# Turning a mixed block behind the value product and adding it two steps later, with the first token's value sent round the scans by GpSimd

## The chip, the cores and the metric

The kernel runs on one core of one Trainium2 chip. The metric is the device time of one execution in microseconds, the median of the runs. The engines are TensorE (PE, its weight loads PEld), VectorE (DVE), ScalarE (ACT), GpSimd (POOL) and SyncE (SP, which here issues all transfers).

## The reference

Two transformer layers over `x` (4 batches of 512 tokens, 512 channels) with a context `ctx` of the same shape. The part that the change touches is the first one, called Mix here, a recurrence over the tokens of each channel:

```
def step(carry, kv_t):               # kt = layernorm(x)[t], vt = ctx[t]
    no = max(o, u + kt); A = exp(o - no); E = exp(u + kt - no)
    y = (A * p + E * vt) / (A * q + E)
    ...
x = x + tanh(g_xattn[0]) * wkv(w, u, layernorm(x), ctx)   # Mix
x = x + tanh(g_ffn[0])   * bitlinear_ffn(layernorm(x))
x = x + tanh(g_xattn[1]) * quantized_cross_attention(layernorm(x), ctx)
x = x + tanh(g_ffn[1])   * quantized_projection(layernorm(x))
```

For the first token p and q are zero, so that y is v of that token itself.

## The kernel before, in words

One program per engine is written out by hand; each engine runs its own list in order, and semaphores connect them (`wait_ge` blocks the engine until another has counted far enough). Mix has 16 steps: step s is batch b = s // 4 and block k = s % 4 of 128 channels. Channels lie on the partitions and the 512 tokens along the free axis, so that the sums over earlier tokens are two scans on VectorE, one for the denominator (`DEN`, L1450) and one for the numerator (`NUM`, L1461). Beside the recurrence each step does work for later stages: TensorE makes a block of the keys (L1062, 12 matmuls into bank 6, "key product") and of the values (L1073, 12 matmuls into bank 7, "value product") of the later cross-attention, and the feed-forward weights are signed on ScalarE and turned by transfers.

What the steps of the prediction touch, in the order in which each engine has it in step s:

- TensorE: `key_turn(s+1)` (L1020, L1022), key product of s, `y_turn(s-1)` (L1041: four transposes of the mixed block `YT` into bank 2), value product of s, `context_turn(s+4)` (L1034: four transposes of a context block into bank 1).
- VectorE: for s up to 7 `batch_stats` (L1365, L1366), `ratio(s-1)` (L1397, L1399, L1403, L1404: the block's quotient into `YT`), scan of `DEN` (L1450), `low_context(s+3)` (L1392), `E*v` (L1455), correction of `DEN` (L1458) and a one for the first token (memset L1459), scan of `NUM` (L1461), `values(s-1)` (L1411: bank 7 to SBUF), correction of `NUM` (L1467) and the first token's v (copy L1468), `residual(s-1)` (L1384: bank 2 added to `X`). Steps 11 to 14 end with parts of the preparation of the next stage (L1417 to L1436).
- ScalarE: two copies of the turned context (L711, L713), the signs of the weights (L771), exponentials (L720, L725), the inverse of `DEN` (L732, L734), the key block to SBUF (L780, L784).
- GpSimd: `normed(s+4)` (L549), `numerators(s+1)` (L540), low half of the key (L580).

The token order is shifted by one: column t of `DEN` and `NUM` belongs to token t+1, and the last column (`SEQ - 1`) to token 0. That column is written by L1459 and L1468, and L1403 moves it to column 0 of `YT`.

Three buffers are single. Bank 7: the value product of s waits for `val_sb`, that is for L1411 of step s, which reads the value product of s-1. Bank 2: `y_turn` waits for the residual (`mixed`) of the block before. `YT`: the last instruction of `ratio(s)` waits until the block before has been turned:

```
up_to(dve, yT_ps, s)          # y_turn(s-1) is done
stt(YT[:, 0:1], ...)          # L1403
stt(YT[:, 1:SEQ], ...)        # L1404
```

Of the kernel before, what the change touches and what calls it, by code (L numbers as in the profile page):

```python
# [8 lines left out]
ALU = mybir.AluOpType  # L9
ACT = mybir.ActivationFunctionType  # L10
# [50 lines left out]
def flamingo_kernel(nc, x, ctx_2048, g_xattn, g_ffn, w, u, w1, w2, w3, wq, bq, wkv, bkv, wp, bp, gamma, wl, out):  # L61
    stack = ExitStack()
    with stack:
# [3 lines left out]
        def sem(name):  # L67
            return stack.enter_context(nc.semaphore(name))
# [158 lines left out]
        logs_done, inv_ready, trial_done, first_done = sem("logs_done"), sem("inv_ready"), sem("trial_done"), sem("first_done")  # L227
# [30 lines left out]
        out_done = sem("out_done")  # L258

        NSMALL = 6  # L260
        CONSTS = {"ones": 3, "growth": 3 + DB, "all": 4 + DB}
        ROUNDED, SUMMED = lambda m, k: DB * m + k + (1 if m == 0 else 2), DB + 1
        SETUP = {"vec_ps": 1, "means_ps": 2, "wl_mean_ps": 3}
# [246 lines left out]
        def _(pool):  # L510
# [23 lines left out]
            def numerators(s):  # L534

                k = s % DB
                pool.wait_ge(ctx_vt, s + 1)
                pool.wait_ge(ue_ready, s + 1)
                up_to(pool, num_set, s - 1)
                nc.gpsimd.tensor_tensor(UEV[k % 2], UE[k % 2], VT[:, k, :], ALU.mult).then_inc(uev_ready, 1)  # L540

            def normed(n):

# [25 lines left out]
            for s in range(DB * BATCH):  # L569
                k = s % DB  # L570
                if k == 0 and s + DB < DB * BATCH:
                    deviations(s // DB + 1)
                if s + DB < DB * BATCH:
                    normed(s + DB)
                if s + 1 < DB * BATCH:
                    numerators(s + 1)
                pool.wait_ge(key_f, s + 1)
                pool.wait_ge(key_hi, s + 1)
                up_to(pool, k_out[k % 2], 16 * (s // 2))
                nc.gpsimd.tensor_tensor(KHL[k % 2][:, 1, :], KF, KHL[k % 2][:, 0, :], ALU.subtract).then_inc(key_lo, 1)  # L580
# [108 lines left out]
        def _(act):  # L689
# [16 lines left out]
            def context(n):  # L706

                b, k = divmod(n, DB)
                act.wait_ge(vT_ps, n + 1)
                up_to(act, val_ps, DB * (b - 1))  # L710
                nc.scalar.copy(CH[b % 2][:, k, :], TURNED(n)[:, :]).then_inc(ctx_hi, 1)  # L711
                up_to(act, num_set, n - DB + 1)
# [14 lines left out]
            def inverse(s):  # L727

                act.wait_ge(den_set, s + 1)
                up_to(act, trial_done, s)  # L730
                up_to(act, first_done, s)
                nc.scalar.activation(INV, DEN[:, :], ACT.Ln).then_inc(logs_done, 1)  # L732
                act.wait_ge(logs_done, s + 1)
                nc.scalar.activation(INV, INV, ACT.Exp, scale=-1.0).then_inc(inv_ready, 1)  # L734

            def magnitudes(s):
                act.wait_ge(signs, s + 1)
# [258 lines left out]
        def _(pe):  # L996
# [54 lines left out]
            for s in range(DB * BATCH):  # L1051
                b, k = divmod(s, DB)
                operands = ((WKVH, CH[b % 2]), (WKVL, CH[b % 2]), (WKVH, CL[b % 2]))
                if s + 1 < DB * BATCH:
                    key_turn(s + 1)
                pe.wait_ge(ctx_hi, DB * b + DB)
                up_to(pe, key_f, s)
                for p, j in parts:
                    if p == 2 and j == 0:
                        pe.wait_ge(ctx_lo, DB * b + DB)  # L1060
                    wt, cx = operands[p]
                    last_ = mm(bank[6][:, :], wt[:, j, k * P:k * P + P], cx[:, j, :],  # L1062
                               start=(p == 0 and j == 0), stop=(p == 2 and j == DB - 1))
                last_.then_inc(key_ps, 1)
                if s > 0:
                    if s == 1:
                        pe.wait_ge(ctx_vt, DB)
                        pe.wait_ge(ctx_lo, DB)
                    y_turn(s - 1)
                up_to(pe, val_sb, s)  # L1070
                for p, j in parts:
                    wt, cx = operands[p]
                    last_ = mm(bank[7][:, :], cx[:, j, k * P:k * P + P], wt[:, j, D:2 * D],  # L1073
                               start=(p == 0 and j == 0), stop=(p == 2 and j == DB - 1))
                last_.then_inc(val_ps, 1)
# [257 lines left out]
        def _(dve):  # L1333
# [60 lines left out]
            def ratio(s):  # L1394

                dve.wait_ge(inv_ready, s + 1)
                tt(DEN[:, :], DEN[:, :], INV, ALU.mult).then_inc(trial_done, 1)  # L1397
                dve.wait_ge(num_set, s + 1)
                tt(Y0, NUM[:, :], INV, ALU.mult).then_inc(first_done, 1)  # L1399
                dve.wait_ge(trial_done, s + 1)  # L1400
                dve.wait_ge(first_done, s + 1)
                up_to(dve, yT_ps, s)
                stt(YT[:, 0:1], DEN[:, SEQ - 1:SEQ], 2.0, Y0[:, SEQ - 1:SEQ], ALU.subtract, ALU.mult)  # L1403
                stt(YT[:, 1:SEQ], DEN[:, 0:SEQ - 1], 2.0, Y0[:, 0:SEQ - 1], ALU.subtract, ALU.mult).then_inc(y_ready, 1)  # L1404

            def values(s):
                dve.wait_ge(val_ps, s + 1)
# [34 lines left out]
            for s in range(DB * BATCH):  # L1442
                k = s % DB
                if s + 2 * DB < DB * BATCH:
                    batch_stats(s // DB + 2, k)
                if s > 0:
                    ratio(s - 1)
                dve.wait_ge(e_ready, s + 1)
                up_to(dve, y_ready, s)
                nc.vector.tensor_tensor_scan(DEN[:, :], DEC[:, k:k + 1].to_broadcast([P, SEQ]), E[:, :], 0.0,  # L1450
                                             ALU.mult, ALU.add).then_inc(sums_done, 1)
                if 0 < s and s + DB - 1 < DB * BATCH:
                    low_context(s + DB - 1)
# [4 lines left out]
                stt(DEN[:, 0:SEQ - 1], DEN[:, 0:SEQ - 1], US[:, k:k + 1], UE[k % 2][:, 1:SEQ], ALU.mult, ALU.add)  # L1458
# [8 lines left out]
                stt(NUM[:, 0:SEQ - 1], NUM[:, 0:SEQ - 1], US[:, k:k + 1], UEV[k % 2][:, 1:SEQ], ALU.mult, ALU.add)  # L1467
                nc.vector.tensor_copy(NUM[:, SEQ - 1:SEQ], VT[:, k, 0:1]).then_inc(num_set, 1)  # L1468
                if s > 0:
                    residual(s - 1)  # L1470
                if s == DB * BATCH - 5:
                    prep_stats(0)
                if s == DB * BATCH - 4:
                    prep_max(0)
                    prep_quant(0)
                    prep_stats(1)
                if s == DB * BATCH - 3:
                    prep_scaled(0)
# [333 lines left out]
```

## Time and profile before

| | |
|---|---|
| median of 3 runs | 966.96 us (964.26 to 967.22) |
| the profiled execution | 966.35 us, its span 964.6 us |
| granted TensorE clock, mean of the span | 0.955 |
| Mix, from the first scan (37.82 us) to the last L1041 (190.46 us) | 152.6 us |

The profiled execution lies 0.6 us under the median; its time is 1.75 us above its span. Positions in the rows below are microseconds from the start of the span.

### The profile page before, as it was taken

To read this page: it belongs to the slowest core of one execution; us is meant where nothing else is said; L and a number is where in the kernel's file an instruction comes from. 1 tells how busy PE (TensorE), PEld (TensorE's weight loads), DVE (VectorE), ACT (ScalarE), POOL (GpSimd) and SP (SyncE) were. 2 spreads that over 40 slices of the span, in tenths; PEclk is the share of its full clock that TensorE was granted. 3 is DMA by queue.
4 is the path that set the end of the run, shared out by engine and by line. 5 is a ranking of instruction groups with operands and counts; after the bars stand their busy time and mean duration, and the time that the engine had idled before them with its cause. 6 is when DMAs were issued, how large, how long until landed. Compare 5 with 4: busy or idle time off the path is not lost.

```text
span 964.6 us, 14534 instructions
## 1 busy us (share of the span) xinstructions
PE 821.9 (85%) x4373; PEld 353.2 (37%) x4373; DVE 759.5 (79%) x1510; ACT 576.9 (60%) x974; POOL 487.2 (51%) x560
## 2 busy tenths in 40 slices
PE   2899987789898989899999968799999999974754
PEld 2544443334344444444444432222223232222321
DVE  4699998879899899999998758477777777634884
ACT  3588886543555565666665544466666666655762
POOL 2866663223334444444444343475757575764761
PEclk9999999899999999999999986899999999996886
DMA  8668875533353442352433241212122221000111
GB/s 283 214 178 221 223 204 151 143 88 65 62 115 55 72 103 57 63 70 55 79 65 65 45 100 54 84 49 79 55 77 57 72 61 46 1 1 0 43 66 66
DMA packets 172392, 86.51 MB, mean 90 GB/s; under 512 B 124048, under 2 KB 156960, under 8 KB 172320
## 3 DMA queue, kind: packets, MB, share of 16 engines
q1 hardware_dynamic: 172320, 85.64, 35.6%
q8 instruction: 34, 0.56, 0.2%
q14 instruction: 38, 0.31, 0.1%
HBM read 37.76 MB, written 12.58 MB: 52 GB/s over the span
## 4 chain that ended last, share of the span: by engine, by line
PE 37%; DVE 22%; issue 7%; ACT 6%; SPq 4%; DMA 3%; POOL 0%; ACTq 0%; DVEq 0%
PE bank L1098 10%; PE bank L1190 5%; PE bank L1161 5%; PE bank L1110 4%; PE bank L1180 4%; DMA A<-B 3%; DVE bank L1516 3%; DVE gsm L1518 3%; DVE B L1527 2%; SPq L438 2%; DVE B L1521 2%; PE bank L1307 2%; ACT bank L806 2%; PE bank L1209 2%; PE bank L1199 2%
## 5 line engine op out<-in xcount | busy, mean ns | idle before, releaser
L1098 PE MATMUL bank<-A,B 128*128 128x512 f16 x1024 | 233.0, 381 | 15.8 <-DVE B L1527 15.6
L1642 DVE TENSOR_REDUCE B<-bank 128x1 f32<-128x512 f32 x256 | 168.0, 683 | 73.9 <-PE bank L1161 73.9
L936 ACT ACTIVATE A<-bank 128x512 f32<-128x512 f32 x256 | 144.1, 593 | 106.9 <-PE bank L1180 103.5
L594 POOL TENSOR_TENSOR B<-B 128x512 f16<-128x512 f32 x64 | 76.4, 1193 | 223.4 <-DVE B L1527 147.2
L1098 PEld LDWEIGHTS bank<-A,B 128*128 128x128 f16 x1024 | 98.8, 98 | 142.9 <-DVE B L1527 20.6
L663 POOL TENSOR_TENSOR B<-A 128x512 f32<-128x512 f32 x64 | 79.3, 1269 | 96.0 <-ACT A L936 96.0
L806 ACT ACTIVATE bank<-B 128x512 f32<-128x512 f32 x64 | 38.5, 602 | 137.4 <-DVE B L1521 137.4
L1110 PE MATMUL bank<-A,B 128*128 128x512 f16 x512 | 120.7, 379 | 0.0
L1180 PE MATMUL bank<-A 98*128 98x512 f16 x256 | 94.5, 390 | 21.2 <-ACT A L936 10.5
L1161 PE MATMUL bank<-A 96*128 96x512 f16 x256 | 97.7, 409 | 7.9 <-DMA A<-B 4.7
L663 POOL TENSOR_TENSOR B<-B,A 128x512 f32<-128x512 f32 x64 | 79.0, 1264 | 0.1
L1190 PE MATMUL bank<-A,B 128*32 128x512 f32 x512 | 69.6, 616 | 1.0 <-ACT A L936 1.0
L1110 PEld LDWEIGHTS bank<-A,B 128*128 128x128 f16 x512 | 49.5, 98 | 54.3 <-DMA B<-B 0.4
L1073 PE MATMUL bank<-B 128*128 128x512 f16 x192 | 47.2, 399 | 17.9 <-DVE B L1411 17.9
L1527 DVE SCALAR_TENSOR_TENSOR B<-bank,gsm 128x512 f32<-128x512 f32 x64 | 44.2, 691 | 16.1 <-ACT bank L806 14.0
L1516 DVE SCALAR_TENSOR_TENSOR bank<-bank,ffs,B 128x512 f32<-128x512 f32 x64 | 48.2, 753 | 9.1 <-PE bank L1098 8.6
L1161 PEld LDWEIGHTS bank<-A 96*128 96x128 f16 x256 | 23.3, 100 | 85.0 <-DVE B L1642 65.3
L801 ACT ACTIVATE B<-bank,ffs 128x512 f32<-128x512 f32 x64 | 43.1, 673 | 13.4 <-PE bank L1098 13.1
L549 POOL TENSOR_SCALAR B<-X,mv,rs 128x128 f32<-128x128 f32 x64 | 49.8, 792 | 0.4
L1180 PEld LDWEIGHTS bank<-A 98*128 98x128 f16 x256 | 25.0, 99 | 67.2 <-ACT A L936 36.6
L1062 PE MATMUL bank<-B 128*128 128x512 f16 x192 | 46.1, 392 | 0.0
L1518 DVE TENSOR_REDUCE gsm<-bank 128x8 f32<-128x512 f32 x64 | 44.3, 692 | 2.2
(216 smaller groups left out, 1479.5 us busy)
## 6 DMA issues: line engine op xcount, KB each, us to landing
B<-in_L_ffn_w_dram SPq DMA_DIRECT2D x48, 256.0 KB, 3.4
A<-k_parts SPq DMA_DIRECT2D x48, 128.0 KB, 2.6
A<-B SPq DMA_DIRECT2D x192, 32.0 KB, 1.9
X<-in_x_dram SPq DMA_DIRECT2D x4, 1024.0 KB, 9.4
B<-in_ctx_dram SPq DMA_DIRECT2D x16, 256.0 KB, 4.4
k_parts<-B SPq DMA_DIRECT2D x16, 256.0 KB, 4.3
v_rows<-B SPq DMA_DIRECT2D x16, 256.0 KB, 2.3
B<-v_rows SPq DMA_DIRECT2D x16, 256.0 KB, 3.4
```

Source lines behind the costliest of these rows:

```text
L594: nc.gpsimd.tensor_tensor(HLb[j][:, 1, :], Db[j % 2], HLb[j][:, 0, :], ALU.subtract).then_inc(lo_done, 1)
L663: nc.gpsimd.tensor_tensor(ACC[j], PR[j] if t == 1 else ACC[j], PR[(HG * t + j) % 8], ALU.add).then_inc(acc_done, 1)
L936: nc.scalar.activation(PR[(HG * t + j) % 8], bank[2 + j % 2][:, :], ACT.Exp, scale=SCALE).then_inc(exp_done, 1)
L1098: last = mm(bank[2 * n + q][:, :], XQT[a][:, m, :], wt[:, m % DB, j * 512:j * 512 + 512], start=(m == 0), stop=(m == 2 * DB - 1))
L1110: last = mm(bank[5 + q][:, :], HT[j][:, m, :], W3T[:, DB * j + m % DB, :], start=(j == 0 and m == 0), stop=(j == FC - 1 and m == 2 * DB - 1))
L1161: mm(bank[ROW_BANKS[r % 3]][:, :], QS[0:96, HG * g + j, t * P:t * P + P], KS[0:96, HG * g + j, :], start=True, stop=True).then_inc(row_ps, 1)
L1180: mm(bank[2 + j % 2][:, :], KS[0:98, HG * g + j, t * P:t * P + P], QS[0:98, HG * g + j, :], start=True, stop=True).then_inc(st_ps, 1)
L1190: last_ = mm(bank[6][DH * j:DH * j + DH, :], VB[:, t, (HG * g + j) * DH:(HG * g + j + 1) * DH], PR[(HG * t + j) % 8], start=(t == 0), stop ...
L1516: stt(H, H, C2, SAb[q], ALU.mult, ALU.mult).then_inc(h_done, 1)
L1518: link(reduce(gsm[:, 0, :], grouped(H), AX.X, ALU.max, apply_absolute_value=True))
L1527: stt(grouped(Db[q]), grouped(bank[q][:, :]), RND, spread(1), ALU.subtract, ALU.mult).then_inc(d_done, 1)
L1642: reduce(NMX[g % 2][:, t, j:j + 1], bank[ROW_BANKS[r % 3]][:, :], AX.X, ALU.max, negate=True).then_inc(row_max, 1)
```

## The change

It does three things. In TensorE's list `y_turn(s-1)` moves from ahead of the value product of step s to behind it. In VectorE's list the residual moves from the end of step s (block s-1) to the place between the correction of `DEN` and the scan of `NUM` (block s-2). And token 0 leaves the scans: the memset L1459, the copy L1468 and the one-column L1403 go; GpSimd writes -v of token 0 into column 0 of `UEV`, and a new `first_value` copies it into `YT` column 0. (`YT` holds -y; the residual multiplies by -tanh.) The remaining operations of `ratio` and `inverse` work on 511 columns in place of 512.

```diff
@@ gpsimd
-                nc.gpsimd.tensor_tensor(UEV[k % 2], UE[k % 2], VT[:, k, :], ALU.mult).then_inc(uev_ready, 1)
+                up_to(pool, y_first, s - 1)
+                nc.gpsimd.tensor_scalar(UEV[k % 2][:, 0:1], VT[:, k, 0:1], -1.0, 0.0, ALU.mult, ALU.add)
+                nc.gpsimd.tensor_tensor(UEV[k % 2][:, LATER], UE[k % 2][:, LATER], VT[:, k, LATER],
+                                        ALU.mult).then_inc(uev_ready, 1)
+            def first_value(s):
+                pool.wait_ge(uev_ready, s + 1)
+                up_to(pool, yT_ps, s)
+                nc.gpsimd.tensor_scalar(YT[:, 0:1], UEV[s % 2][:, 0:1], 1.0, 0.0, ALU.mult, ALU.add).then_inc(y_first, 1)
...
+                if s > 0:
+                    first_value(s - 1)
                 if s + DB < DB * BATCH:
                     normed(s + DB)
@@ tensor
             def y_turn(s):
                 pe.wait_ge(y_ready, s + 1)
+                pe.wait_ge(y_first, s + 1)
...
-                if s > 0:
-                    ...
-                    y_turn(s - 1)
                 up_to(pe, val_sb, s)
                 for p, j in parts:
...
                 last_.then_inc(val_ps, 1)
+                if s > 0:
+                    ...
+                    y_turn(s - 1)
                 if s + DB < DB * BATCH:
                     context_turn(s + DB)
@@ vector
-                tt(DEN[:, :], DEN[:, :], INV, ALU.mult).then_inc(trial_done, 1)
+                tt(DEN[:, PAIRED], DEN[:, PAIRED], INV[:, PAIRED], ALU.mult).then_inc(ratio_done, 1)
...
                 up_to(dve, yT_ps, s)
-                stt(YT[:, 0:1], DEN[:, SEQ - 1:SEQ], 2.0, Y0[:, SEQ - 1:SEQ], ALU.subtract, ALU.mult)
-                stt(YT[:, 1:SEQ], DEN[:, 0:SEQ - 1], 2.0, Y0[:, 0:SEQ - 1], ALU.subtract, ALU.mult).then_inc(y_ready, 1)
+                stt(YT[:, LATER], DEN[:, PAIRED], 2.0, Y0[:, PAIRED], ALU.subtract, ALU.mult).then_inc(y_ready, 1)
...
-                nc.vector.memset(DEN[:, SEQ - 1:SEQ], 1.0).then_inc(den_set, 1)
+                if s > 1:
+                    residual(s - 2)
                 dve.wait_ge(ev_ready, s + 1)
                 nc.vector.tensor_tensor_scan(NUM[:, :], ...
...
-                nc.vector.tensor_copy(NUM[:, SEQ - 1:SEQ], VT[:, k, 0:1]).then_inc(num_set, 1)
-                if s > 0:
-                    residual(s - 1)
...
             ratio(DB * BATCH - 1)
+            residual(DB * BATCH - 2)
```

TensorE's list in one step of Mix before, from the end of the key product on (bank 6 key product, bank 2 `y_turn`, bank 7 value product, bank 1 context):

```order
L1062 MATMUL bank6<-B 128x512 [waits ctx_lo]
L1062 MATMUL bank6<-B 128x512 x3
L1041 MATMUL bank2<-id32,B 128x128 [waits mixed,y_ready]
L1041 MATMUL bank2<-id32,B 128x128 x3
L1073 MATMUL bank7<-B 128x512 [waits val_sb]
L1073 MATMUL bank7<-B 128x512 x11
L1034 MATMUL bank1<-id32,B 128x128 [waits ctx_lo,ctx_vt,ctx_in2]
L1034 MATMUL bank1<-id32,B 128x128 x3
```

The same place of the change (its L1077, L1083, L1056 and L1048 are the L1062, L1073, L1041 and L1034 of before; these rows are shown without bank numbers):

```order
L1077 MATMUL bank<-B 128x512 [waits ctx_lo]
L1077 MATMUL bank<-B 128x512 x3
L1083 MATMUL bank<-B 128x512 [waits val_sb]
L1083 MATMUL bank<-B 128x512 x11
L1056 MATMUL bank<-id,B 128x128 [waits mixed,y_first,y_ready]
L1056 MATMUL bank<-id,B 128x128 x3
L1048 MATMUL bank<-id,B 128x128 [waits ctx_lo,ctx_vt,ctx_in2]
L1048 MATMUL bank<-id,B 128x128 x3
```

The four transposes of y have moved behind the value product, and so behind its wait for `val_sb`.

VectorE's list in one step before, from the end of `ratio` to the residual:

```order
L1403 SCALAR_TENSOR_TENSOR B<-bank,B 128x1 [waits yT_ps,first_done,trial_done]
L1404 SCALAR_TENSOR_TENSOR B<-bank,B 128x511
L1450 SCALAR_TENSOR_TENSOR bank<-vec,bank 128x512 [waits y_ready,e_ready]
L1392 TENSOR_TENSOR B<-bank,B 128x512 [waits ctx_vt,ctx_hi]
L1455 TENSOR_TENSOR bank<-bank,B 128x512 [waits ctx_vt]
L1458 SCALAR_TENSOR_TENSOR bank<-bank,vec,B 128x511 [waits ue_ready,sums_done]
L1459 MEMSET bank 128x1
L1461 SCALAR_TENSOR_TENSOR bank<-vec,bank 128x512 [waits ev_ready]
L1411 SCALAR_TENSOR_TENSOR B<-bank,bv_all 128x512 [waits val_ps]
L1467 SCALAR_TENSOR_TENSOR bank<-bank,vec,B 128x511 [waits uev_ready,scans_done]
L1468 COPY bank<-B 128x1
L1384 SCALAR_TENSOR_TENSOR X<-bank,ffs,X 128x4x128 [waits yT_ps]
```

The same place of the change (L1417 is the L1404 of before, L1399 the residual L1384, L1424 the L1411):

```order
L1417 SCALAR_TENSOR_TENSOR B<-bank,B 128x511 [waits yT_ps,ratio_done]
L1463 SCALAR_TENSOR_TENSOR bank<-vec,bank 128x512 [waits y_ready,e_ready]
L1407 TENSOR_TENSOR B<-bank,B 128x512 [waits ctx_vt,ctx_hi]
L1468 TENSOR_TENSOR bank<-bank,B 128x512 [waits ctx_vt]
L1471 SCALAR_TENSOR_TENSOR bank<-bank,vec,B 128x511 [waits ue_ready,sums_done]
L1399 SCALAR_TENSOR_TENSOR X<-bank,ffs,X 128x4x128 [waits yT_ps]
L1476 SCALAR_TENSOR_TENSOR bank<-vec,bank 128x512 [waits ev_ready]
L1424 SCALAR_TENSOR_TENSOR B<-bank,bv_all 128x512 [waits val_ps]
L1482 SCALAR_TENSOR_TENSOR bank<-bank,vec,B 128x511 [waits uev_ready,scans_done]
```

Three one-column instructions are gone and the residual stands ahead of the scan of `NUM`; the wait for `yT_ps` at the end of `ratio` is still there.

## Rows read from the trace of the kernel before

**Rows 1.** Busy time by stretch, steps 2 to 12: PE, PEld, DVE, ACT, POOL, clock
```profile
51.97:150.75 98.78, 89.36 (x478) 48.27 (x476) 94.93 (x172) 81.45 (x126) 60.91 (x71) 1.00 0.77 207
```

**Rows 2.** Waits of Mix: who waited for whom, total us, times, longest
```profile
PE bank L1073 <- DVE B L1411: 17.9, 14, 3.6
```

**Rows 3.** Timeline of one step: start, us, engine, line, operation, idle time and its releaser
```profile
106.67 0.67 DVE L1411 SCALAR_TENSOR_TENSOR B<-bank,bv_all 128x512 f32<-128x512 f32 x1
...
107.41 2.76 PE L1073 MATMUL bank<-B 128*128 128x512 f16 x12 [1.05 <-DVE B L1411]
...
107.92 0.15 DVE L1468 COPY bank<-B 128x1 f32<-128x1 f32 x1
107.98 0.74 DVE L1384 SCALAR_TENSOR_TENSOR X<-bank,ffs,X 128x512 f32<-128x512 f32 x1
...
108.64 0.69 DVE L1397 TENSOR_TENSOR bank<-bank,B 128x512 f32<-128x512 f32 x1
...
109.79 0.57 PEld L1034 LDWEIGHTS bank<-id,B 128*128 128x128 f32 x4
110.00 0.60 PE L1034 MATMUL bank<-id,B 128*128 128x128 f32 x4
110.02 0.16 DVE L1403 SCALAR_TENSOR_TENSOR B<-bank,B 128x1 f32<-128x1 f32 x1
110.09 0.68 DVE L1404 SCALAR_TENSOR_TENSOR B<-bank,B 128x511 f32<-128x511 f32 x1
110.33 1.16 POOL L580 TENSOR_TENSOR B<-B 128x512 f16<-128x512 f32 x1 [3.06 <-ACT B L780]
...
110.64 0.58 ACT L711 CAST B<-bank 128x512 f16<-128x512 f32 x1 [0.44 <-PE bank L1034]
...
111.12 0.59 ACT L713 COPY B<-bank 128x512 f32<-128x512 f32 x1
...
112.01 0.67 DVE L1392 TENSOR_TENSOR B<-bank,B 128x512 f16<-128x512 f32 x1
...
113.86 1.22 DVE L1461 TENSOR_TENSOR_SCAN bank<-vec,bank 128x512 f32<-128x512 f32 x1
113.89 0.06 DVE L1459 MEMSET bank<- 128x1 f32 x1
...
114.99 0.67 DVE L1411 SCALAR_TENSOR_TENSOR B<-bank,bv_all 128x512 f32<-128x512 f32 x1
```

**Rows 4.** Timeline, VectorE, the step before: with the statistics of a later batch
```profile
97.56 0.67 DVE L1411 SCALAR_TENSOR_TENSOR B<-bank,bv_all 128x512 f32<-128x512 f32 x1
...
98.86 0.74 DVE L1384 SCALAR_TENSOR_TENSOR X<-bank,ffs,X 128x512 f32<-128x512 f32 x1
...
100.34 0.67 DVE L1397 TENSOR_TENSOR bank<-bank,B 128x512 f32<-128x512 f32 x1
```

**Rows 5.** Timeline, VectorE: L1411 of steps 1, 11 to 14, and step 13's start
```profile
51.97 0.67 DVE L1411 SCALAR_TENSOR_TENSOR B<-bank,bv_all 128x512 f32<-128x512 f32 x1
...
141.61 0.67 DVE L1411 SCALAR_TENSOR_TENSOR B<-bank,bv_all 128x512 f32<-128x512 f32 x1
...
150.75 0.67 DVE L1411 SCALAR_TENSOR_TENSOR B<-bank,bv_all 128x512 f32<-128x512 f32 x1
...
154.99 0.69 DVE L1425 TENSOR_REDUCE gsm<-B 128x8 f32<-128x512 f32 x1 [2.20 <-ACT B L749]
...
159.10 0.68 DVE L1404 SCALAR_TENSOR_TENSOR B<-bank,B 128x511 f32<-128x511 f32 x1
...
163.41 0.67 DVE L1411 SCALAR_TENSOR_TENSOR B<-bank,bv_all 128x512 f32<-128x512 f32 x1
...
172.90 0.67 DVE L1411 SCALAR_TENSOR_TENSOR B<-bank,bv_all 128x512 f32<-128x512 f32 x1
```

**Rows 6.** Timeline, TensorE: matmuls after a longer wait, in Mix and behind it
```profile
164.13 4.12 PE L1073 MATMUL bank<-B 128*128 128x512 f16 x12 [3.64 <-DVE B L1411]
...
205.90 3.63 PE L1098 MATMUL bank<-A,B 128*128 128x512 f16 x16 [1.78 <-DVE B L1527]
```

More of the change, by code:

```diff
@@ L226, in flamingo_kernel @@
         sums_done, den_set, num_set = sem("sums_done"), sem("den_set"), sem("num_set")
-        logs_done, inv_ready, trial_done, first_done = sem("logs_done"), sem("inv_ready"), sem("trial_done"), sem("first_done")
+        logs_done, inv_ready, ratio_done, y_first = sem("logs_done"), sem("inv_ready"), sem("ratio_done"), sem("y_first")
         y_ready, yT_ps, mixed = sem("y_ready"), sem("yT_ps"), sem("mixed")
@@ L260, in flamingo_kernel @@
         NSMALL = 6
+        LATER = slice(1, SEQ)
+        PAIRED = slice(0, SEQ - 1)
         CONSTS = {"ones": 3, "growth": 3 + DB, "all": 4 + DB}
@@ L586, in _ @@
                     prep_lo(0)
+            first_value(DB * BATCH - 1)
             def lo_part(i, j):
@@ L711, in context @@
                 nc.scalar.copy(CH[b % 2][:, k, :], TURNED(n)[:, :]).then_inc(ctx_hi, 1)
-                up_to(act, num_set, n - DB + 1)
+                up_to(act, ev_ready, n - DB + 1)
+                up_to(act, uev_ready, n - DB + 1)
                 nc.scalar.copy(VT[:, k, :], TURNED(n)[:, :]).then_inc(ctx_vt, 1)
@@ L729, in inverse @@
                 act.wait_ge(den_set, s + 1)
-                up_to(act, trial_done, s)
-                up_to(act, first_done, s)
-                nc.scalar.activation(INV, DEN[:, :], ACT.Ln).then_inc(logs_done, 1)
+                up_to(act, ratio_done, 2 * s)
+                nc.scalar.activation(INV[:, PAIRED], DEN[:, PAIRED], ACT.Ln).then_inc(logs_done, 1)
                 act.wait_ge(logs_done, s + 1)
-                nc.scalar.activation(INV, INV, ACT.Exp, scale=-1.0).then_inc(inv_ready, 1)
+                nc.scalar.activation(INV[:, PAIRED], INV[:, PAIRED], ACT.Exp, scale=-1.0).then_inc(inv_ready, 1)
             def magnitudes(s):
@@ L1064, in _ @@
                 last_.then_inc(key_ps, 1)
-                if s > 0:
-                    if s == 1:
-                        pe.wait_ge(ctx_vt, DB)
-                        pe.wait_ge(ctx_lo, DB)
-                    y_turn(s - 1)
                 up_to(pe, val_sb, s)
@@ L1075, in _ @@
                 last_.then_inc(val_ps, 1)
+                if s > 0:
+                    if s == 1:
+                        pe.wait_ge(ctx_vt, DB)
+                        pe.wait_ge(ctx_lo, DB)
+                    y_turn(s - 1)
                 if s + DB < DB * BATCH:
@@ L1396, in ratio @@
                 dve.wait_ge(inv_ready, s + 1)
-                tt(DEN[:, :], DEN[:, :], INV, ALU.mult).then_inc(trial_done, 1)
+                tt(DEN[:, PAIRED], DEN[:, PAIRED], INV[:, PAIRED], ALU.mult).then_inc(ratio_done, 1)
                 dve.wait_ge(num_set, s + 1)
-                tt(Y0, NUM[:, :], INV, ALU.mult).then_inc(first_done, 1)
-                dve.wait_ge(trial_done, s + 1)
-                dve.wait_ge(first_done, s + 1)
+                tt(Y0[:, PAIRED], NUM[:, PAIRED], INV[:, PAIRED], ALU.mult).then_inc(ratio_done, 1)
+                dve.wait_ge(ratio_done, 2 * s + 2)
                 up_to(dve, yT_ps, s)
-                stt(YT[:, 0:1], DEN[:, SEQ - 1:SEQ], 2.0, Y0[:, SEQ - 1:SEQ], ALU.subtract, ALU.mult)
-                stt(YT[:, 1:SEQ], DEN[:, 0:SEQ - 1], 2.0, Y0[:, 0:SEQ - 1], ALU.subtract, ALU.mult).then_inc(y_ready, 1)
+                stt(YT[:, LATER], DEN[:, PAIRED], 2.0, Y0[:, PAIRED], ALU.subtract, ALU.mult).then_inc(y_ready, 1)
             def values(s):
@@ L1457, in _ @@
                 dve.wait_ge(ue_ready, s + 1)
-                stt(DEN[:, 0:SEQ - 1], DEN[:, 0:SEQ - 1], US[:, k:k + 1], UE[k % 2][:, 1:SEQ], ALU.mult, ALU.add)
-                nc.vector.memset(DEN[:, SEQ - 1:SEQ], 1.0).then_inc(den_set, 1)
+                stt(DEN[:, PAIRED], DEN[:, PAIRED], US[:, k:k + 1], UE[k % 2][:, LATER], ALU.mult,
+                    ALU.add).then_inc(den_set, 1)
+                if s > 1:
+                    residual(s - 2)
                 dve.wait_ge(ev_ready, s + 1)
@@ L1466, in _ @@
                 dve.wait_ge(uev_ready, s + 1)
-                stt(NUM[:, 0:SEQ - 1], NUM[:, 0:SEQ - 1], US[:, k:k + 1], UEV[k % 2][:, 1:SEQ], ALU.mult, ALU.add)
-                nc.vector.tensor_copy(NUM[:, SEQ - 1:SEQ], VT[:, k, 0:1]).then_inc(num_set, 1)
-                if s > 0:
-                    residual(s - 1)
+                stt(NUM[:, PAIRED], NUM[:, PAIRED], US[:, k:k + 1], UEV[k % 2][:, LATER], ALU.mult,
+                    ALU.add).then_inc(num_set, 1)
                 if s == DB * BATCH - 5:
```

## The prediction

> **What bounds the kernel now.** I read the busy time by stretch first, then the waits of Mix, then the timeline of one step, because the change touches Mix alone, the first fifth of the span. In steps 2 to 12 VectorE is busy 94.93 of 98.78 us, 96%, with TensorE at its upper clock of 2.4 GHz (granted 1.00) [rows 1]; the reader is to see that there is nearly no gap on VectorE, and that a step lasts as long as VectorE's list: 98.78 / 11 = 8.98 us on average. The waits say how TensorE hangs on it: the value product L1073 waited 14 times for L1411, VectorE's copy of the value product before it [rows 2]. The timeline shows it once: L1411 starts at 106.67, L1073 at 107.41 after an idle time of 1.05 us [rows 3]. So the value product starts 0.74 us after L1411, whenever TensorE itself would be ready.
>
> **The change part by part.**
>
> *What goes from VectorE.* Three one-column instructions a step. Their price is not their duration but what they push the next start back: L1468 at 107.92, the next at 107.98: 0.06 us; L1403 at 110.02, L1404 at 110.09: 0.07 us; the memset runs inside the scan that starts 0.03 us before it, and costs nothing [rows 3]. Together 0.13 us a step. The residual is moved, not removed: L1384 at 107.98, the next at 108.64, 0.66 us at either place [rows 3].
>
> *The wait that is moved into VectorE's path.* The last instruction of `ratio` (L1404) waits for `yT_ps`, the turn of the block before, as that turn still reads `YT`. Before, this turn ran ahead of the value product and was long done. Now it stands behind it, and the value product starts only after L1411. So there is a ring of one step: L1411 of step s, value product of s, `y_turn(s-1)`, L1404 of step s+1, the rest of VectorE's list, L1411 of step s+1. Its terms:
>
> - L1411 to the value product: 107.41 - 106.67 = 0.74 us [rows 3].
> - Value product and the four transposes behind it: the context's turn stands there before and has the same shape, its last transpose ends at 110.00 + 0.60 = 110.60, so 110.60 - 107.41 = 3.19 us [rows 3].
> - Release: ScalarE's L711 started 0.04 us after that end (110.64) [rows 3]. So L1404 can start 0.74 + 3.19 + 0.04 = 3.97 us after L1411.
> - L1404 to the next L1411: 114.99 - 110.09 = 4.90 us, and the residual, which now stands in this part: 4.90 + 0.66 = 5.56 us [rows 3].
>
> The ring takes 9.53 us. VectorE itself would come to L1404 earlier: before, 110.09 - 106.67 = 3.42 us after L1411, less 0.66 (residual gone from here) and 0.13, so 2.63 us; in the steps with statistics it is 0.82 us more, 3.45 (98.86 to 100.34 is 1.48, in place of 0.66) [rows 3, 4]. Both are below 3.97. VectorE would stand still at L1404 for 0.5 us in the one kind of step and 1.3 us in the other, and the scan of `DEN` stands behind the waiting instruction. Then for the scan of `NUM`, L1411 and so the next value product all is late: nothing catches it up.
>
> The ring holds from L1411 of step 1 (51.97) to that of step 12 (150.75), eleven times: 11 x 9.53 = 104.8 us in place of 98.8 [rows 5], **+6.0 us**. Bounds: with a release of 0.00 to 0.15 us in place of 0.04 it is +5.6 to +7.3.
>
> *Step 12 to 13* (12.66 us before [rows 5]) is set by the preparation: L1425 waits for ScalarE until 154.99. That chain begins with transfers of step 11, so I let it keep its distance from L1411 of step 11: 154.99 - 141.61 = 13.38 [rows 5]; L1411 of step 12 comes 9.53 after that of step 11, so L1425 3.85 behind it. From there to L1404 4.11 - 0.07, and to L1411 163.41 - 159.10 = 4.31, plus the residual 0.66 [rows 5]: 12.86, **+0.2 us**. If the chain moves with step 12 instead, +0.6.
>
> *Step 13 to 14* (9.49 us [rows 5]): here TensorE had waited 3.64 us and its value product took 4.12 us [rows 6]. It waits no less now. L1404 comes after 0.72 (163.41 to 164.13) + 4.12 + the transposes 0.81 (109.79 to 110.60) + 0.04 = 5.69 us, and L1411 4.31 + 0.66 later: 10.66, **+1.2 us** [rows 3, 5, 6]. Lower bound: at full speed (2.76) L1404 would not wait here, -0.1; upper bound: all 12 matmuls as slow as the slower ones may add one more us, +2.2.
>
> *Steps 14 and 15*: the preparation at the end of step 14 stands between L1411 and L1404, and I take it to cover the turn; only the 0.13 us are left, **-0.2 us** in all. Steps 0 and 1 have no block to turn ahead of L1404, 0.
>
> *GpSimd.* Two one-column instructions more a step. They are no longer than the 512-column L580 (1.16 us), so 2.3 us at most, under the 3.06 us that GpSimd stood idle ahead of L580 in the step [rows 3]. First value's own wait is for the turn that ends 3.93 us after L1411; L580 ends 111.49 - 106.67 = 4.82 after it. Price 0. At the tail the added residual of block 14 runs while block 15 is turned. Price 0.
>
> *Sum*: 6.0 + 0.2 + 1.2 - 0.2 = 7.2 us onto the profiled execution's 966.35: 973.6. The median lies 0.6 above it: **974.2 us**. Its own range, from the bounds of the terms (5.6 + 0.2 - 0.1 - 0.2 to 7.3 + 0.6 + 2.2 - 0.2, and 1 us to either side, for the runs before lie within 3 us): 971.5 to 977.9.
>
> **The rivals.**
>
> *The turn is hidden after all and VectorE gains* (the other side). If y is turned before VectorE comes to L1404, only the 0.13 us are left, in 15 steps 2.0 us: 965.0, which is no measurable difference. It decides at 2.63 us after L1411 (3.45 with statistics), where the rows give 3.97. For it: TensorE comes to the value product 0.8 us earlier, as y no longer stands ahead of it. Against it: the value product was not waiting for TensorE but for L1411 [rows 2], and its 12 matmuls alone end at 109.79 or later, 3.1 us after L1411 [rows 3].
>
> *The context's copies are late instead.* The context's turn stands behind y's now, 0.81 us later at most. It ends 0.74 + 3.19 + 0.81 = 4.74 after L1411, then L711 0.04, 0.48 to L713, 0.59 for it: 5.85 us [rows 3]. L1392 wants it 3.97 + (112.01 - 110.09) = 5.89 after L1411. That is a tie. If it is late by 0.3 us, 11 steps cost 3.3 us more, 977.5. Against it: the slack, though only 0.04 us, is there, and 0.81 for the turn is its upper end.
>
> *TensorE's clock falls in each step.* Its idle time grows: 1.05 us in a step of 9.11 (97.56 to 106.67) becomes about 1.05 + 9.53 - 9.11 = 1.5 us [rows 3, 4]. After 3.64 us idle the value product took 4.12, after 1.05 us 2.76 [rows 3, 6]: 1.36 us more, times 11, is 15 us: 989. Against it: after 1.78 us idle, 16 matmuls took 3.63 us, 0.227 each, as 2.76 / 12 = 0.230 [rows 3, 6]. The Trainium skill ("TensorE: Matmul & The Clock Gate", "A second HAM failure mode: psum-queue depth-cycling") speaks for this rival: it says that often repeated short idle times between groups of matmuls can make the clock go back and forth between its two levels. By it the time would be the 989; no row here has such a repeated idle time with a fallen clock, and in rows 1 it stayed at 1.00 through eleven idle times of about 1 us.
>
> **How the numbers follow.** The forecast 0.82; late copies beside it 0.07 (977.5); the clock 0.04 (989); hidden 0.05 (965.0); the rest something that I don't see, 0.02. A difference of 0.3% (2.9 us) is about what a measurement of this kernel can tell from none. The forecast's range, stretched to the late copies, holds about 0.88, less its own uncertainty: 971 to 978.5. Slower by over 0.3%: 0.82 + 0.07 + 0.04 less a little, 0.91. Within 0.3%: the hidden turn and the forecast's low end, 0.06. Faster: 0.03.
>
> **What would show it.** Right, if in the timeline after, the last instruction of `ratio` has idle time ahead of it that ends with the transposes of y, 0.5 us in steps with statistics and 1.3 us without, and L1411 to L1411 is 9.5 us from step 1 to 12. TensorE's wait for L1411 should be longer (1.5 us). The late copies show as idle time ahead of `low_context` that ends with the second copy of the context (L713); the clock as under 1.00 in that stretch. Wrong, if VectorE shows no idle time at `ratio`: then the value product doesn't wait for L1411 as I think, or the turn overtakes it.

## The result and the profile after

The change made the kernel slower: 975.82 us (median of 4 runs, 974.27 to 977.14) against 965.61 us (4 runs of the kernel before, 963.9 to 967.22), a ratio of 1.0111 [1.0094, 1.0129]. The prediction said 974.2 with a range of 971 to 978.5. The profiled execution took 977.14 us with a span of 975.2, which is 10.6 us more than the span of before. The lines of before have new numbers: L1411 is now L1424, L1404 is L1417, the residual L1384 is L1399, L1397 is L1412, the scan of `DEN` L1450 is L1463, L1425 is L1438; on TensorE L1073 is L1083, L1041 is L1056, L1034 is L1048.

The windows of the kernel after, from L1424 of step 1 to that of step 12 (us, then PE, PEld, DVE, ACT and POOL busy, then granted clock; the last two numbers are of the transfers):

```profile
51.90:158.06 106.16, 88.93 (x475) 47.19 (x473) 93.66 (x139) 81.60 (x126) 64.42 (x93) 1.00 0.71 194
```

Beside [rows 1]: the eleven steps take 106.16 us in place of 98.78, VectorE has less work in them (93.66 in place of 94.93), and it stands still for 12.5 us where it had 3.85. The clock stayed at 1.00. Who waits is in the waits of Mix in the kernel after (total us, times, longest):

```profile
PE bank L1083 <- DVE B L1424: 29.2, 15, 5.7
DVE B L1417 <- PE bank L1056: 11.1, 11, 2.1
```

The first line answers to [rows 2], 17.9 us there. The second line is new: the last operation of `ratio` waits for the turn of y, L1056. The timeline of the kernel after, TensorE and VectorE, shows one such step; it answers to [rows 3]:

```profile
109.68 0.67 DVE L1424 SCALAR_TENSOR_TENSOR B<-bank,bv_all 128x512 f32<-128x512 f32 x1
...
113.01 0.60 PE L1056 MATMUL bank<-id,B 128*128 128x128 f32 x4
...
113.72 0.69 DVE L1417 SCALAR_TENSOR_TENSOR B<-bank,B 128x511 f32<-128x511 f32 x1 [1.52 <-PE bank L1056]
114.88 1.23 DVE L1463 TENSOR_TENSOR_SCAN bank<-vec,bank 128x512 f32<-128x512 f32 x1 [0.46 <-DVE B L1417]
...
119.64 0.67 DVE L1424 SCALAR_TENSOR_TENSOR B<-bank,bv_all 128x512 f32<-128x512 f32 x1
120.37 2.76 PE L1083 MATMUL bank<-B 128*128 128x512 f16 x12 [1.90 <-DVE B L1424]
...
122.97 0.60 PE L1056 MATMUL bank<-id,B 128*128 128x128 f32 x4
123.69 0.69 DVE L1417 SCALAR_TENSOR_TENSOR B<-bank,B 128x511 f32<-128x511 f32 x1 [1.53 <-PE bank L1056]
129.24 0.68 DVE L1424 SCALAR_TENSOR_TENSOR B<-bank,bv_all 128x512 f32<-128x512 f32 x1
```

Follow the ring in the last five rows: L1424 at 119.64, value product 0.73 later, the transposes end at 123.57, L1417 starts 0.12 behind that, and the next L1424 comes at 129.24, 9.60 us after the first. Nine of the eleven steps take 9.60 or 9.61. The other two take 9.75 and 9.96; the step of 9.96 is the one from 109.68, in which the scan L1463 started 0.46 us late behind L1417.

What lies behind step 12 is in the next rows of the timeline, which answer to [rows 5, 6]:

```profile
162.49 0.69 DVE L1438 TENSOR_REDUCE gsm<-B 128x8 f32<-128x512 f32 x1 [3.10 <-ACT B L763]
...
166.47 0.69 DVE L1417 SCALAR_TENSOR_TENSOR B<-bank,B 128x511 f32<-128x511 f32 x1
171.42 0.67 DVE L1424 SCALAR_TENSOR_TENSOR B<-bank,bv_all 128x512 f32<-128x512 f32 x1
...
172.15 5.21 PE L1083 MATMUL bank<-B 128*128 128x512 f16 x12 [5.74 <-DVE B L1424]
...
177.90 0.69 DVE L1417 SCALAR_TENSOR_TENSOR B<-bank,B 128x511 f32<-128x511 f32 x1 [2.12 <-PE bank L1056]
...
182.86 0.67 DVE L1424 SCALAR_TENSOR_TENSOR B<-bank,bv_all 128x512 f32<-128x512 f32 x1
...
185.26 0.77 DVE L1441 TENSOR_SCALAR gsm<-gsm 128x8 f32<-128x8 f32 x1
...
200.55 0.74 DVE L1399 SCALAR_TENSOR_TENSOR X<-bank,ffs,X 128x512 f32<-128x512 f32 x1
201.44 1.08 PE L1056 MATMUL bank<-id,B 128*128 128x128 f32 x4 [2.22 <-DVE X L1399]
```

The account of the 10.6 us, from L1424 to L1424: eleven steps +7.4, step 12 to 13 +0.7 (13.36 in place of 12.66), 13 to 14 +1.95 (11.44 in place of 9.49), 14 to 15 +0.4, the tail up to the first feed-forward operation on VectorE +0.4, all else about -0.2.

### The profile page after: what moved, and what is told of

It reads as the page before. It is cut to its first block, busy times and chain, and to the rows that moved or that the text cites. A ratio compares the mean times of both kernels' runs of the same rounds, so it can differ in the third digit from the quotient of the medians.

```text
span 975.2 us, 14557 instructions
## 1 busy us (share of the span) xinstructions
PE 819.9 (84%) x4373; PEld 352.3 (36%) x4373; DVE 757.8 (78%) x1462; ACT 577.3 (59%) x974; POOL 493.3 (51%) x592
## 4 chain that ended last, share of the span: by engine, by line
PE 43%; DVE 30%; issue 10%; ACT 7%; SPq 5%; DMA 5%; DVEq 0%; ACTq 0%
PE bank L1113 10%; PE bank L1205 5%; PE bank L1176 5%; PE bank L1125 4%; PE bank L1195 4%; PE bank L1083 4%; DMA A<-B 3%; DVE bank L1530 3%; DVE gsm L1532 3%; DVE B L1541 2%; SPq L440 2%; DVE B L1535 2%; PE bank L1322 2%; ACT bank L820 2%; PE bank L1224 2%
## 5 line engine op out<-in xcount | busy, mean ns | idle before, releaser
L1083 PE MATMUL bank<-B 128*128 128x512 f16 x192 | 48.3, 406 | 29.2 <-DVE B L1424 29.2
L1077 PE MATMUL bank<-B 128*128 128x512 f16 x192 | 46.1, 392 | 0.0
```

## Experiments

The theory under test is the ring: L1424, value product, turn of y, L1417, L1424. Rivals: VectorE's own list (the residual's new place costs something), and another chain that is nearly as long. Each ratio is to runs of the kernel before on the same chip (medians 965.31, 964.03 and 965.97 us in the three groups, in the order e1 to e4, e5 to e9, e10 and e11).

**Lengthen the ring: the context's turn ahead of y's (e4).** If the ring holds, one more set of four transposes in it costs their time in each step.

```diff
-                if s > 0:
-                    ...
-                    y_turn(s - 1)
                 if s + DB < DB * BATCH:
                     context_turn(s + DB)
+                if s > 0:
+                    ...
+                    y_turn(s - 1)
```

> The change with the context's turn ahead of y's turn, one buffer for y. Ring theory: the turn of y ends later by the context's four transposes, 0.5 to 0.7 us, all of which goes into each of the steps 1 to 12: 5 to 8 us slower than the change, 981 to 984 us, with VectorE's idle time ahead of the end of ratio longer by that. The rival that the late context copies bound the steps says that it gets faster than the change (under 975).

Measured: 981.24 us, 1.0165 [1.0150, 1.0180], at the lower end of what was expected. The timeline of e4:

```profile
60.87 4.45 PE L1083 MATMUL bank<-B 128*128 128x512 f16 x12 [1.98 <-DVE B L1424]
...
101.98 0.67 DVE L1424 SCALAR_TENSOR_TENSOR B<-bank,bv_all 128x512 f32<-128x512 f32 x1
...
105.31 0.60 PE L1048 MATMUL bank<-id,B 128*128 128x128 f32 x4
105.75 0.60 PE L1056 MATMUL bank<-id,B 128*128 128x128 f32 x4
106.46 0.69 DVE L1417 SCALAR_TENSOR_TENSOR B<-bank,B 128x511 f32<-128x511 f32 x1 [0.79 <-PE bank L1056]
112.02 0.67 DVE L1424 SCALAR_TENSOR_TENSOR B<-bank,bv_all 128x512 f32<-128x512 f32 x1
```

y's transposes start 0.44 us after the context's, and the step grows from 9.60 to 10.04, by the same 0.44. So the turn of y is in the ring, with its full price. Nine of the eleven steps take 10.04 or 10.05 us, and the step of 9.96 has become 10.40. The eleventh takes 11.72 (60.14 to 71.86): its value product took 4.45 us in place of 2.76, at a granted 0.62 from 60.87 to 65.32, behind a wait of 1.98 us. The nine other waits of 1.97 to 2.33 us in these steps left the clock at 1.00 (71.86 to 162.58); behind the next one, 1.98 us, the value product at 163.31 took 4.45 again. So the clock rival, which the eleven steps of the change do not show, begins to show here.

**Cut the ring: two buffers for y (e2), and the context's turn ahead as well (e3).** With two `YT` L1417 waits for the turn of one block earlier. VectorE's list of operations stays as in the change. GpSimd's first value and TensorE's turn use the two buffers in the same way; those lines are left out here.

```diff
-        YT, INV, Y0, IOTA = T32[:, 4, :], T32[:, 5, :], T32[:, 6, :], T32[:, 7, :]
+        YT, INV, Y0, IOTA = [T32[:, 4, :], T32[:, 7, :]], T32[:, 5, :], T32[:, 6, :], T32[:, 7, :]
...
-                up_to(dve, yT_ps, s)
-                stt(YT[:, LATER], ...
+                up_to(dve, yT_ps, s - 1)
+                stt(YT[s % 2][:, LATER], ...
```

> The change with two buffers for y (the second in the place of the token numbers that are used only at the start), so that the end of ratio waits for the turn two blocks back. Ring theory: the idle time of VectorE ahead of the end of ratio goes to 0. But the context's turn still stands behind y's turn: from L1424 to low_context at least 4.37 (its end in the trace after) + 0.03 + 0.48 + 0.59 + 0.1 = 5.57 us, and 3.63 on to the next L1424, a second ring of 9.2 us. So 11 x (9.6 - 9.2) = 4.5 and some 2 us of steps 13 and 14 come back: about 969 us, with VectorE's idle time now ahead of low_context. The rival that only the turn of y counts says 964.

> Two buffers for y, and the context's turn ahead of y's turn, both still behind the value product. Both rings are open: VectorE's own list bounds the steps again, 963 to 966 us, with less than 0.2 us idle a step ahead of ratio's end and ahead of low_context. If the place behind the value product costs in another way (the clock, the bank of the residual), it stays above 968.

Measured: e2 969.05 us, 1.0035 [1.0023, 1.0047], as expected; e3 967.86 us, 1.0038 [1.0021, 1.0056], 2 us above the upper end of what was expected, and by the ratios it can't be told from e2. Neither has a wait at L1417 any more. The waits and the timeline of e2 say what came next:

```profile
DVE bank L1412 <- ACT B L748: 4.7, 7, 1.5
...
DVE B L1407 <- ACT B L728: 2.1, 5, 0.8
```

```profile
120.12 0.60 PE L1048 MATMUL bank<-id,B 128*128 128x128 f32 x4
...
121.24 0.59 ACT L728 COPY B<-bank 128x512 f32<-128x512 f32 x1
121.92 0.69 DVE L1407 TENSOR_TENSOR B<-bank,B 128x512 f16<-128x512 f32 x1
```

L1407 (`low_context`) starts 0.09 us after ScalarE's second copy of the context: the prediction's second rival, hidden while the longer ring held. This step took 9.21 us (L1424 at 116.36 and 125.57). In e3 that is nearly gone (0.8 us in 2 waits), but L1412, the first operation of `ratio`, now waits 6.1 us in 7 waits for ScalarE's inverse L748. That third chain I had not seen.

**Undo the move of the turn alone (e1).** `y_turn(s-1)` stands ahead of the value product again; the bypass and the residual's new place stay.

```diff
+                if s > 0:
+                    ...
+                    y_turn(s - 1)
                 up_to(pe, val_sb, s)
                 ...
-                if s > 0:
-                    ...
-                    y_turn(s - 1)
```

> The change with one part undone: y is turned ahead of the value product again; the later residual and GpSimd's first value stay. The ring theory (L1411, value product, turn of y, end of ratio) says that this alone makes the loss: VectorE doesn't stand still at the end of ratio, a step is 0.13 us shorter than before, and with 0.4 us lost at the tail the time is about 1.5 us under before, 963 to 965.5 us. The rival, that the residual's new place or GpSimd's added work costs, says that half or more of the loss stays: 970 us or more.

Measured: 970.48 us, 1.0048 [1.0032, 1.0064]. The move of the turn accounts for 1.0111 to 1.0048, about 6 us, but the rest of the change is not the gain that I expected (963 to 965.5 us). It costs 4 to 5 us, and the measured time is on the side of the rival (970 us or more). The wait at L1417 is gone, and steps without another wait take 8.91 us. Yet others take 10.16 or 9.62. The timeline of e1, L1424 of three steps with SyncE's queue (SPq) and ScalarE between them:

```profile
59.55 0.68 DVE L1424 SCALAR_TENSOR_TENSOR B<-bank,bv_all 128x512 f32<-128x512 f32 x1
60.26 0.35 SPq L376 DMA_DIRECT2D v_rows<-B  x1
...
60.65 5.15 SPq L368 DMA_TRANSPOSE A<-B  x3
...
67.05 1.49 ACT L785 ACTIVATE B<-B 128x1536 f16<-128x1536 f32 x1 [2.45 <-DMA A<-B]
...
68.48 0.67 DVE L1424 SCALAR_TENSOR_TENSOR B<-bank,bv_all 128x512 f32<-128x512 f32 x1
...
71.76 0.70 DVE L1412 TENSOR_TENSOR bank<-bank,B 128x511 f32<-128x511 f32 x1 [1.13 <-ACT B L748]
...
78.64 0.68 DVE L1424 SCALAR_TENSOR_TENSOR B<-bank,bv_all 128x512 f32<-128x512 f32 x1
```

This is a second ring, two steps long (19.09 us from 59.55 to 78.64). The store of the values, L376, waits on SyncE's queue for L1424. The transposing transfers of the weights, L368, stand behind it on the same queue, though they need nothing from it. ScalarE waits 2.45 us for them before it takes the signs (L785), the inverse L748 stands behind the signs in its list, and VectorE's `ratio` waits for the inverse. L1424 of step s so sets L1424 of step s+2. In this ring VectorE's part from L1412 to L1424 is 78.64 - 71.76 = 6.88 us; before it was 114.99 - 108.64 = 6.35 [rows 3]. The residual's new place puts 0.66 us into it; the removed one-column instruction takes a part of that back.

**The bypass alone, with the residual back at the end of the step (e7).** This is e1 with this edit:

```diff
-                if s > 1:
-                    residual(s - 2)
                 dve.wait_ge(ev_ready, s + 1)
...
+                if s > 0:
+                    residual(s - 1)
...
-            residual(DB * BATCH - 2)
```

Two smaller edits belong to the bypass, though the section on the change does not name them: ScalarE's second copy of the context (L728) waits for `ev_ready` and `uev_ready` in place of `num_set`, and the two products of `ratio` are counted in one semaphore in place of two, which is one wait less on VectorE. They are in every run with the bypass.

> The first token's way round the scans by GpSimd alone: y is turned ahead of the value product and the residual of block s-1 stands at the end of the step, both as before. After the run with y ahead (970.5 us, VectorE waiting 7 times and 6.0 us for the inverse ahead of ratio) the theory is a second ring: L1411, the store of the values, the weights' transfers, signs, inverse, ratio, the scans, L1411, over two steps; the residual's new place put 0.66 us into its VectorE part (L1397 to L1411). With the residual outside again the waits ahead of ratio fall to about those of before (1.3 us) and the 0.13 to 0.2 us a step are gained: 962.5 to 965.5 us. The rival that GpSimd's added work or the 511 columns cost says 968 us or more.

Measured: 963.41 us, 0.9993 [0.9977, 1.0008]: no difference that can be told. Its free steps take 8.91 and 8.12 us where before has 9.11 and 8.32, so the bypass was worth 0.20 us a step. What hides the gain is the second ring, more of it than I expected: L1412 waited for L748 three times, 3.2 us in all.

**Cut the second ring: weights ahead of the stores on SyncE's queue.** The same edit was put on e1 (e8) and on the change (e9).

```diff
-                if s > 0:
-                    stores(s - 1)
                 turn_weights(s)
+                if s > 0:
+                    stores(s - 1)
```

> The change with y ahead of the value product again, and in SyncE's list the weights' transposes of a step ahead of the stores of keys and values, so that they don't wait for L1411 any more. Second-ring theory: the signs' wait for the transposes falls by about 2 us a step, VectorE doesn't wait ahead of ratio, and the steps are as long as VectorE's own list (8.9 us with statistics, 8.1 to 8.3 without): 961 to 965 us. If the residual's place costs in another way, it stays at 968 to 971.

> The change as it is, with the weights' transposes ahead of the stores in SyncE's list. The two rings are apart: the ring through the turn of y does not pass SyncE, so its steps stay at 9.6 us; only the two longer steps (9.75 and 9.96) and step 12 to 13, which hangs on the weights' transfers, gain 0.5 and 1 to 1.5 us: 973 to 975.5 us. If the weights' ring was what made the change slow, it comes back to under 968.

Measured: e8 965.73 us, 1.0002 [0.9984, 1.0020], by the ratios 0.46% (4.4 us) under e1 though 0.7 us above the range expected; e9 972.52 us, 1.0086 [1.0064, 1.0108], 0.5 under the range expected. In e8 no wait ahead of L1412 is left in the eleven steps, and they take 8.90 to 8.93 us with statistics or a part of the preparation, 8.77 or 8.78 without. The steps without could be shorter, as in e7; there L1407 waits for the context's copy again (1.9 us in 4 waits). The residual's new place lies in that ring too, between L1407 and L1424: e11 below, with the residual outside, has no such wait in these steps, and they take 8.12 us. And of the 3.6 us by which its last L1424 comes ahead of that of before (184.09, 187.66), 1.5 are lost by the first feed-forward operation on VectorE (194.33, 196.36). The runs of e1, e3 and e8 spread over 7 to 8 us, those of the other experiments over 1 to 5, but for e5 (13 us); I have no cause for it. Between the medians of e8 and e9, which differ by the place of the turn alone and ran on one chip, lie 6.8 us: the price of the move without the second ring. In e9 the steps keep the 9.60 of the y ring, as they must if that is what holds them; its waits:

```profile
DVE B L1417 <- PE bank L1056: 13.5, 12, 2.3
DVE gsm L1438 <- ACT B L763: 1.6, 1, 1.6
```

The wait at L1438 halves (3.1 to 1.6): that chain too began at SyncE's queue. The step of 9.75 is gone, that of 9.96 is not.

**The move of the turn alone, on the kernel before (e5).** The residual stays at the end of the step, and so waits for a turn that has just begun.

```diff
-                if s > 0:
-                    ...
-                    y_turn(s - 1)
                 up_to(pe, val_sb, s)
                 ...
+                if s > 0:
+                    ...
+                    y_turn(s - 1)
```

> The kernel before with y turned behind the value product and nothing else: the residual of block s-1 still ends step s and waits for that turn. Ring theory: L1411 to the residual 0.74 + 3.19 + 0.11 = 4.04 us, 0.66 for it, 0.82 for statistics, 6.35 from L1397 to the next L1411: 11.9 us a step with statistics and 11.05 without, in place of 9.0: 28 us in steps 1 to 12 and some 8 behind them, 995 to 1003 us, VectorE's idle time now ahead of the residual. So the later residual would be what keeps the change's loss small.

Measured: 1020.63 us, 1.0540 [1.0488, 1.0593], at least 17 us more than expected. The place is right, the size is not. The timeline of e5, and the granted clock (the third number from the end) in two stretches of it:

```profile
63.47 0.67 DVE L1411 SCALAR_TENSOR_TENSOR B<-bank,bv_all 128x512 f32<-128x512 f32 x1
64.20 4.43 PE L1068 MATMUL bank<-B 128*128 128x512 f16 x12 [3.73 <-DVE B L1411]
68.47 0.60 PE L1041 MATMUL bank<-id,B 128*128 128x128 f32 x4
69.11 0.75 DVE L1384 SCALAR_TENSOR_TENSOR X<-bank,ffs,X 128x512 f32<-128x512 f32 x1 [4.24 <-PE bank L1041]
...
76.93 0.67 DVE L1411 SCALAR_TENSOR_TENSOR B<-bank,bv_all 128x512 f32<-128x512 f32 x1
...
155.20 4.21 PE L1068 MATMUL bank<-B 128*128 128x512 f16 x12 [2.92 <-DVE B L1411]
...
167.87 2.76 PE L1068 MATMUL bank<-B 128*128 128x512 f16 x12 [2.92 <-DVE B L1411]
```

```profile
64.20:68.40 4.20, 4.20 (x12) 1.64 (x13) 0.67 (x2) 1.23 (x3) 2.81 (x4) 0.59 0.57 128
68.40:77.60 9.20, 5.53 (x33) 3.05 (x30) 8.26 (x15) 6.25 (x10) 2.72 (x3) 1.00 0.56 157
```

With the residual in the ring, TensorE waits 3.7 us in a step, and the value product that follows runs at a granted 0.59 (a mix of the upper level, 1.00, and the lower, 0.50), 4.43 us in place of 2.76; the ring carries that too (13.46 us a step from 63.47 to 76.93). Six steps have such a value product (4.43 to 4.45 us). The later ones show that the length of the last wait alone does not decide: behind 2.92 us it took 4.21 us once and 2.76, full speed, twice (the two last rows, and at 178.86); behind 0.81 and 1.94 us with 1.04 us of matmuls between it took 2.76. So the clock rival of the prediction is real. The waits of 1.5 to 1.9 us that the change makes did not bring it about in its trace, but 0.44 us more, in e4, did so twice. And the two parts of the change belong together: the turn behind the value product without the residual's move costs five times as much (5.4% in place of 1.1%).

**The queue order alone (e10), and with the bypass (e11).** The edit of e8, on the kernel before and on e7.

> The kernel before with nothing changed but SyncE's list: the weights' transposes ahead of the stores. Second-ring theory: that ring is open, and in the steps without statistics VectorE no longer waits ahead of ratio (1.3 us in all), which were 9.0 and 8.5 us in place of 8.32; steps with statistics stay at 9.11. Some 1.3 to 2 us in steps 8 to 11 and about 1.5 in step 12 to 13: 961 to 964 us. A rival: VectorE's list bounds all of Mix before, no difference.

> The first token's way round the scans alone (y ahead of the value product, residual at the end of the step), and the weights' transposes ahead of the stores. All three rings (turn of y, weights, context) leave VectorE's list free: 8.9 us a step with statistics, 8.1 to 8.2 without, 11 steps in about 95.5 us in place of 98.8 and 98.9 in the run of the bypass alone; 958.5 to 961.5 us. If a step without statistics stays at 8.8, the context's copies bound it, and the time is 962 to 964.

Measured: e10 962.03 us, 0.9972 [0.9959, 0.9984]; e11 961.88 us, 0.9965 [0.9952, 0.9979], 0.4 above what was expected. Both beat the kernel before and the changed one; they can't be told from each other. The timeline of e10 shows the ring cut:

```profile
114.71 0.67 DVE L1411 SCALAR_TENSOR_TENSOR B<-bank,bv_all 128x512 f32<-128x512 f32 x1
116.67 0.69 DVE L1397 TENSOR_TENSOR bank<-bank,B 128x512 f32<-128x512 f32 x1
118.32 0.47 SPq L374 DMA_DIRECT2D v_rows<-B  x1
119.63 1.50 ACT L771 ACTIVATE B<-B 128x1536 f16<-128x1536 f32 x1
121.16 3.81 SPq L366 DMA_TRANSPOSE A<-B  x3
123.03 0.67 DVE L1411 SCALAR_TENSOR_TENSOR B<-bank,bv_all 128x512 f32<-128x512 f32 x1
```

L771 has no idle time ahead of it, and none of the eleven steps waits at `ratio`: they take 9.11 or 8.32 us. In e11 Mix is shorter still (8.91 and 8.12; the first feed-forward operation on VectorE at 190.2 in place of 193.2). But these 3 us don't reach the end, where the two spans are 959.4 and 959.5 us. Half of them goes in the feed-forward stage; its windows, first e11, then e10:

```profile
190.20:550.30 360.10, 341.75 (x1753) 161.03 (x1752) 321.20 (x684) 202.62 (x357) 143.10 (x227) 1.00 0.36 68
```

```profile
193.20:551.80 358.60, 340.42 (x1754) 160.09 (x1753) 321.50 (x685) 202.73 (x357) 143.21 (x227) 1.00 0.37 69
```

The same work takes 1.5 us more there, and TensorE is busy for 1.33 us more. The clock fell once in e11: from 300.00 to 305.00 it was 0.66, and behind a wait of 2.53 us 16 matmuls took 1.86 us and the next eight 2.57. In e10 the clock stayed at 1.00, and the same matmuls, behind 2.38 us, took 1.05 and 1.89. That is the 1.5 us. How the rest is lost behind 550 us I did not follow.

## Why the prediction was right, and where its terms were off

The time came out nearer than the sum. The forecast stood on the 966.96 us of the runs before it, and the runs beside the change gave 965.61. Of the 10.2 us measured the sum had 7.2, and the higher base hid 1.35 of what was missing; that part is luck. Every term of the sum came out above its forecast.

**The ring** is shown: it appears where the prediction put it, grows by 0.44 us when 0.44 us is put into it (e4), and goes when it is cut (e1, e2). Its term was 6.0 us and came out at 7.4; the idle time at L1417 was mostly 0.7 us in steps with statistics and 1.5 without, forecast 0.5 and 1.3. Of the 1.4 us, 0.8 is the release: TensorE's last transpose ended 0.11 to 0.12 us before L1417, where I had taken 0.04 from a copy on ScalarE; 11 x 0.07. The range given (0.00 to 0.15) held it. The rest is the two steps of 9.75 and 9.96. The first waited for L748, and is gone in e9: the second ring. The second has 0.46 us of idle time at the scan L1463 with only its own engine's L1417 named as releaser; e1, e4, e8 and e9 have such a wait too; e2, e3, e7 and e11 have none. It is always 0.46 us at the scan that opens step 8, and the change and these four share one list on VectorE. The kernel before, e5 and e10, which share another list, have such a line at another place, 0.53 us at L1403 in step 1 (45.0 to 45.3). So it goes with a place in VectorE's list and not with the ring; why it is there is open.

**Step 12 to 13**: the upper value was the right one. L1438 came 4.43 us after L1424, not 3.85: ScalarE's chain doesn't keep its distance from step 11 but moves on with the late steps. From there to L1424 it took 3.98 and 4.95 us, forecast 4.04 and 4.97.

**Step 13 to 14**: I took the cold value product (cold: at the lower clock) at 4.12 us; it took 5.21, behind an idle time of 5.74 us in place of 3.64, and nearly all of it ran at the lower clock (a granted 0.50 from 172.10 to 177.00, where 164.10 to 168.20 had 0.66 before). That is the upper bound, near enough. That the longer wait is the reason is not shown: in e9 a wait of 4.23 us at this place gave 5.30.

**Steps 14 and 15**: the 0.2 us of the removed instructions came, but L1441, a small operation of the preparation, took 0.77 us in place of 0.17. It ran from 185.26 to 186.03, beside GpSimd's low half of the key, which ran from 184.84 to 186.00; in the kernel before, this operation ended just as GpSimd's began. The other runs bear this out: in e4, e9 and e11 too L1441 begins inside that GpSimd operation and ends 0.01 to 0.03 us behind it (0.85, 0.77 and 1.00 us), and in e1, e2, e3, e7, e8 and e10 nothing runs beside it and it takes 0.17. No run separates the two in another way.

**The tail**, put at 0, cost 0.4: I wrote that the added residual of block 14 runs while block 15 is turned. It can't, since the turn waits for that residual to free bank 2 [the row at 201.44, idle 2.22 us for L1399]. I had that buffer in the list of single buffers and did not apply it to the last step.

**The removed instructions**: 0.20 us a step in the free steps of e7 and e11, not 0.13. What I missed is that `ratio`'s last part also starts 0.08 us sooner, now that one wait less stands ahead of it and no one-column operation comes first; which of the two does it is not shown (188.87 to 189.65 before, for L1399 to L1403, is 0.78; now 0.70 from L1414 at 187.15 to L1417 at 187.85). In the changed kernel all of it disappears in the wait.

**The rivals.** That the turn is hidden was wrong: 11 waits at L1417, ten of them in the eleven steps. The late context copies did not show in steps 2 to 12 of the change, but e2 and e8 show them at once when the ring is cut, as the tie of 5.85 to 5.89 us had said. The clock stayed at 1.00 in the eleven steps, with idle times of 1.5 to 1.9 us in each but the first. The Trainium skill's rule that the prediction cited ("TensorE: Matmul & The Clock Gate", "A second HAM failure mode: psum-queue depth-cycling") did not come true at that length. Its picture, a clock that goes back and forth between two levels, is what e5 shows at 3.7 us, and e4 twice behind 1.98 us.

## What to carry to other kernels

Before an instruction is moved behind another one's wait, close the ring: follow each single buffer that it frees back to the engine for which the wait stands, and add up the loop; if it is longer than the busiest engine's list, it is the new step. Do the same for the last step, where nothing stands behind to cover. And where several chains are nearly as long as the step, a gain on one shows as a wait on the next: the gain that was to be had here (0.28%, or 0.35% with the bypass, which can't be told apart) lay not in VectorE's list but in a queue, where transfers that needed nothing stood behind a store that waited.

## What the runs showed of the hardware

- A repeated idle time of TensorE of 1.5 to 1.9 us ahead of the value product in each step of 9.6 us left the clock at 1.00 over 106 us. At 1.97 to 2.33 us in steps of 10 us it fell behind two of eleven such waits (e4). One of 3.7 us in each step of 13.5 us brought the matmuls behind it to about 0.6, and the clock was back at 1.00 in the rest of each step (e5). Waits of equal length, 2.92 us, gave 4.21 us once and 2.76 twice (e5).
- A one-column instruction on VectorE records 0.15 or 0.16 us but pushes the next start back by only 0.06 to 0.08 us; taking three of them out of a step, with one wait, gave 0.20 us (e7, e11).
- A 128x8 operation on VectorE (L1441) that began inside GpSimd's L593 (128x512, 1.16 us) ended with it, 0.77 to 1.00 us after its start, in four runs; with nothing beside it it took 0.17 us.
